# Straight code for the middle batches of a vision tower, and one GpSimd step moved behind a Newton step

## The reference, cut to what matters

```python
# 1 token mixer
y = sigmoid(q) * (ew @ (exp(k) * v)) / (ew @ exp(k))
h = y @ out_w + out_b + x
h = (h - mean) * rsqrt(var + 1e-5) * ln_g + ln_b      # first norm: scale ln_g, offset ln_b
h = concat([cls_tok, h])                              # a class row in front of the 256 tokens
# 2 attention with 16 heads, whose probabilities are mixed over the heads and normalised
attn = softmax(q @ k.T * scale)
attn = einsum('bhij,hg->bgij', attn, reattn_w)
attn = (attn - mean_over_heads) * rsqrt(var_over_heads + 1e-3) * gamma + beta
h = h + (attn @ v) @ w_out + b_out                    # q, k, v from layernorm(h)
# 3 feed-forward with ternary weights and activations rounded to 8 bits
h = h + bitlinear(silu(bitlinear(ln(h), w_gate)) * bitlinear(ln(h), w_up), w_down)
```

## Time and profile before

| | |
|---|---|
| median of three runs | 874.68 us |
| the profiled execution, its own time | 874.84 us |
| its span, first to last instruction | 873.1 us |
| mean granted TensorE clock | 0.935 of full speed |
| busy: PE, DVE, ACT, POOL | 84%, 74%, 50%, 21% of the span |
| instruction packets on the two instruction queues | 18 and 16 |

### The profile page before, as it was taken

One profiled execution on the slowest core, in us unless ns is written; L12 is line 12 of the kernel. 1 busy time (PEld: TensorE's weight loads), 2 busy tenths in 40 slices (PEclk: granted clock), 3 DMA queues, 4 the chain that ended last, 5 costly groups with the idle time before them and its releaser, 6 DMA issues.

```text
span 873.1 us, 14228 instructions
## 1 busy us (share of the span) xinstructions
PE 732.1 (84%) x4514; PEld 527.8 (60%) x4514; DVE 642.9 (74%) x1442; ACT 435.2 (50%) x1198; POOL 179.6 (21%) x367
## 2 busy tenths in 40 slices
PE   1769688989998999898998999899998899788754
PEld 0446466757675777666775767477766677456521
DVE  1596758688958896888768885889688886868444
ACT  0103637563657364745747265836575574747210
POOL 0308124012310233013301231023301330013000
PEclk9959799989999999989998999899999999899877
DMA  8300410050003200230004000311023000500000
GB/s 330 129 1 0 172 46 2 17 175 9 31 1 129 72 30 0 85 107 12 24 28 164 6 30 0 128 64 36 0 73 119 13 1 28 166 7 7 1 12 0
DMA packets 25414, 49.26 MB, mean 56 GB/s; under 512 B 2715, under 2 KB 6052, under 8 KB 24740
## 3 DMA queue, kind: packets, MB, share of 16 engines
q1 hardware_dynamic: 24340, 45.34, 15.4%
q10 hardware_dynamic: 1040, 3.49, 1.0%
HBM read 13.16 MB, written 2.11 MB: 17 GB/s over the span
## 4 chain that ended last, share of the span: by engine, by line
PE 37%; issue 26%; DVE 16%; ACT 8%; POOL 8%; DMA 4%; POOLq 1%; SPq 0%; ACTq 0%; DVEq 0%
PE small L535 5%; PE big L535 5%; PE small L686 5%; PE big L552 5%; DMA pg<-pst 4%; PE big L618 4%; DVE pst L1186 3%; DVE mx L1193 2%; ACT pst L918 2%; PE big L716 2%; PE small L641 2%; PE small L671 2%; ACT ot L1007 2%; DVE var L1221 1%; POOL nww L1569 1%
## 5 line engine op out<-in xcount | busy, mean ns | idle before, releaser
L918 ACT ACTIVATE pst<-big,nb 128x256 f32<-128x256 f32 x256 | 117.7, 473 | 46.9 <-DVE nb L1196 24.5
L618 PEld LDWEIGHTS big<-w_mix,pg 128*128 128x128 f32 x1024 | 122.5, 194 | 25.9 <-DVE an L1265 18.3
L618 PE MATMUL big<-w_mix,pg 128*128 128x128 f32 x1024 | 126.3, 279 | 7.9 <-DVE an L1265 7.9
L1193 DVE TENSOR_REDUCE mx<-big 128x4 f32<-128x1024 f32 x64 | 78.2, 1222 | 26.2 <-PE big L552 25.7
L552 PE MATMUL big<-qk_t 64*128 64x256 f32 x512 | 72.6, 402 | 20.1 <-ACT qk_t L901 20.1
L939 ACT ACTIVATE sqb<-big 128x1024 f32<-128x1024 f32 x64 | 64.8, 1014 | 42.9 <-PE big L618 42.9
L1221 DVE TENSOR_REDUCE var<-sqb 128x64 f32<-128x1024 f32 x64 | 77.6, 1213 | 9.1 <-ACT sqb L939 9.1
L1265 DVE TENSOR_TENSOR an<-big,rstd 128x1024 f32<-128x1024 f32 x64 | 78.4, 1225 | 2.7 <-DVE rstd L1252 0.2
L1186 DVE TENSOR_SCALAR pst<-pst,rr 128x256 f32<-128x256 f32 x256 | 72.8, 350 | 0.0
L552 PEld LDWEIGHTS big<-qk_t 64*128 64x128 f32 x512 | 44.2, 186 | 45.6 <-ACT qk_t L901 27.9
L535 PE MATMUL small<-xnt,w_qkv 128*128 128x256 f32 x256 | 65.5, 400 | 0.0
(11 more groups left out here) (200 smaller groups left out, 1233.5 us busy)
## 6 DMA issues: line engine op xcount, KB each, us to landing
pg<-pst SPq DMA_DIRECT2D x128, 256.0 KB
w_qkv<-in_w_qkv SPq DMA_DIRECT2D x1, 3072.0 KB
xt<-in_x_t SPq DMA_DIRECT2D x8, 256.0 KB, 2.9
xr<-in_x_tok SPq DMA_DIRECT2D x8, 256.0 KB, 2.7
out<-h SPq DMA_DIRECT2D x16, 128.0 KB
an<-in_gate_t ACTq DMA_DIRECT2D x1, 1024.0 KB, 8.5
an<-in_up_t ACTq DMA_DIRECT2D x1, 1024.0 KB, 10.8
an<-in_down_t ACTq DMA_DIRECT2D x1, 1024.0 KB, 13.3
```

The costliest lines, as they stand in the source:

```text
L618: last = mm(mix_place(n)[:, i * P:(i + 1) * P], pg[:, hf * (IB // 2) + i, it * T + jt * P:it * T + (jt + 1) * P], w_mix[:], start=True, st ...
L918: last = A(pst[:, g % 2, h % GH, it, :], big[p % 2][:, (j * TT + it) * T:(j * TT + it + 1) * T], ACT.Exp, bias=nb[:, h, it:it + 1], scale= ...
L1193: V.reduce_max(mx[:, hs, :], big[p % 2][:, :].rearrange("p (h t l) -> p h t l", h=2, t=TT), AX)\
```

## The change

The five hardware loops become Python loops, so that the instructions of iterations 1 to 5 (on SP 1 to 4) are written out, with constants in place of registers. On POOL, g and b leave `mixer_out` for a function of their own, `mixer_affine`. It is called for batch b + 1 behind `newton(b, 0)`, where it stood for batch b + 2 at the end of iteration b. Batch 0 keeps its place in the setup.

```diff
-            with sp.Fori(1, B - 3) as b:
+            for b in range(1, B - 3):
                 iteration(b, True, True)
...
-            with pe.Fori(1, B - 2) as b:
+            for b in range(1, B - 2):
                 iteration(b, True, True)
...
             def mixer_out(b):
                 power(b, pool_a, dve_a, ve_a, rs_a, P, slice(0, TT), "ve")
+
+            def mixer_affine(b):
                 pool.wait_ge(dve_a.sem, dve_a.at(b, ("n", 1)))
                 G.tensor_tensor(h2[:], h2[:], tok_g[:].unsqueeze(1).to_broadcast([P, TT, M]), ALU.mult)\
                     .then_inc(pool_a.sem, 1)
...
                 for n in mixes:
                     newton(b, n)
-                    if n == 3 and do_scores:
+                    if n == 0 and do_scores:
+                        mixer_affine(b + 1)
+                    elif n == 3 and do_scores:
                         mixer_norm(b + 1)
...
             mixer_out(0)
+            mixer_affine(0)
             mixer_norm(0)
```

More of the change, by code:

```diff
@@ L1073, in _ @@
             iteration(0, True, True)
-            with act.Fori(1, B - 2) as b:
+            for b in range(1, B - 2):
                 iteration(b, True, True)
@@ L1496, in _ @@
             iteration(0, True, True)
-            with dve.Fori(1, B - 2) as b:
+            for b in range(1, B - 2):
                 iteration(b, True, True)
@@ L1653, in _ @@
             iteration(0, True, True)
-            with pool.Fori(1, B - 2) as b:
+            for b in range(1, B - 2):
                 iteration(b, True, True)
```

## The result

The changed kernel takes 883.54 us (median of 14 runs, 877.12 to 1080.16) where the kernel before takes 875.76 (median of 14). The ratio is 1.0072, with a 95% interval of 1.0052 to 1.0092: slower by about 6.3 us (4.6 to 8.1). The two medians by themselves lie 7.8 apart, inside that interval. The forecast was 879.5, with a range of 875.0 to 884.0.

The account below looks back on a forecast made before the run. At the seam between iterations PE was taken to wait on a chain through DVE, POOL and ACT. Straight code -2.4, hold-off +5.75 and clock +1.53 gave +4.88 us: 879.5 against the median, range 875.0 to 884.0.

Parts of the forecast that it names:

- the hold-off: Block 0 at seams before iterations 1 to 6: g, issued first, holds off DVE's `rstd`; 5.75 us in all, chance 0.80.
- PE's wait: Ahead of PE's block 3 at the seam: the wait grows from 1.05 us to about 2.
- lateness at the seam is priced in full: Between iterations: block 3 later by 1.53 us makes the next `an` later by the whole 1.53; nothing is absorbed.
- Iteration 0: Its start: y * y begins 1.03 us sooner without g and b ahead; the hold on `rstd` takes it to 0.0.
- The straight code: Five iterations leaving the loop: less register arithmetic ahead of waits, 2.4 us saved; bounds 0 and 4.8.
- The third piece: From the start of `rstd` to `an`: straight code saves 0.11 us, only as long as `rstd` is short.
- The first piece: From the first `an` to that of block 7: 24.43 us in the loop, 24.15 straight, saving 0.28.
- The second: From block 7 to the next first `an`: 70.03 us in the loop, 69.83 straight, saving 0.20.
- The clock: At the seams, ahead of PE's block 3: one further fall, 1.53 us; bounds none and four (6.1).
- The rival by which a taken branch costs a fetch: Loop seams: the loop hid more than straight pieces show, over 2 us for each iteration needed; chance 0.03.
- the 0.90 and 0.91 of the forecast: Start of `hq` to `rstd`: 0.90 us with a taken branch, 0.91 where the loop is left; branch worth nothing.
- fetching straight code stalls: Rival on the written-out iterations: fetching their code stalls an engine, making the kernel slower; chance 0.02.

Follow-up runs that it names:

- e3: Changed kernel plus a wait that lets g go only when `rstd` of block 0 has ended: 876.35 us, 1.0001 to the kernel before.
- e1: Kernel before with all five loops written out, g and b left where they were: 876.68 us, 1.0002 to the kernel before.
- e4: Changed kernel with g and b each as two instructions of 128 x 256 values: 878.43 us, 1.0033 to the kernel before.
- e9: Changed kernel with g and b behind the Newton step of block 1, not block 0: 881.54 us, 1.0067 to the kernel before.
- e5: e3 plus a second wait, letting block 7's `rstd` go ahead of POOL's copy: 877.28 us, 1.0013 to the kernel before.
- e2: Changed kernel with the five hardware loops kept, so the moved step alone: 883.98 us, 1.0090 to the kernel before.
- e13: Changed kernel plus twelve unread 128 x 512 products on PE per iteration from 1 on: 879.05 us, 1.0048 to the kernel before.
- e10: e1 plus twelve unread 128 x 512 products on PE per iteration from 1 on: 870.44 us, 0.9952 to the kernel before.
- e11: e10 plus five more unread products between the gate and the up projection: 868.00 us, 0.9914 to the kernel before.
- e12: Kernel before, loops kept, plus twelve unread 128 x 512 products on PE per iteration from 1 on: 870.50 us, 0.9943 to it.

## Why the prediction was right, and where it was not

- **The place, the cause and the size of the hold-off: right.** 1.28 us was forecast for `rstd` and 1.27 measured, 0.07 behind g where 0.08 was forecast; 1.31 from `rstd` to `an`, and 316.83 - 315.53 = 1.30 measured. g holds alone; b costs `an` and POOL's queue nothing. Undoing it (e3) gave back 6.2 us, against the 5.75 of the sum. The traces of the changed kernel and e1 say the same: from the start of the first `rstd` to the second `an` of an iteration it takes 1.31 + 4.89 = 6.20 us with the hold and 0.26 + 4.99 = 5.25 without, so 0.95 at each of six seams, with 1.03 in iteration 0 some 6.7 in all. Lateness at the seam is thus carried on all but for 0.10.
- **PE's wait: about 2 us forecast, 1.80 measured.** That lateness at the seam is priced in full holds but for the 0.10 for block 0 (e3, e4), and less closely for block 1 (e9). It does not carry over to block 7 (e5), where the earlier trace rows show the same hold: there the hold, 0.8 us longer than `rstd` alone, has no price that can be measured.
- **Iteration 0: right.** `y` ends at 124.40 and y * y now starts at 124.48, 0.08 behind it and not 1.11, and the hold takes that back. The first `an` is 0.39 later than before, of which `y` itself came 0.37 later, out of the setup.
- **The straight code: mis-sized, -2.4 forecast, 0 measured** (1.0002, 0.9976 to 1.0028, so between 2.1 us less and 2.5 more). The third piece, 0.11 between `rstd` and `an`, is lost again by the next `an` (e1), as said above. The first piece came: 24.16 us from the first `an` to block 7 in the changed kernel, for 24.43. The second, 0.20 behind block 7, did not: in the profiled executions of before and after that stretch is longer in each of iterations 0 to 5, by 0.9 to 1.2 us in four of them and by 2.1 and 2.5 in 1 and 5, where the fall of the clock grew; the hold at the next seam is 0.94 of it. The piece had been read from iteration 0 alone, at equal clock by choice, while the clock there was the one thing that would not stay equal.
- **The clock: the wrong place, and for a reason that did not hold.** One fall more at a seam, 1.53 us, was in the sum, because PE's wait there would double. The wait grew to 1.80, and in the profiled execution no seam has a fall. The falls behind block 7 grew in iterations 1 and 5 instead, 48 to 51 us in all. In e2 the falls came at three seams, and in e1 and e3, with the shortest wait, at one. What the clock does is thus an outcome of each version's timing that these rows could not give; the runs of one kernel already spread by 0.925 to 0.940.
- **The fetches.** The rival by which a taken branch costs a fetch that straight code gives back is out at the size that it needed, over 2 us for each iteration: 1.0002 in e1. A fetch of some tenths of a microsecond at four seams is too small for that ratio to show; against it stand only the 0.90 and 0.91 of the forecast. That fetching straight code stalls is not seen either: the packets rose from 18 and 16 to 36 and 28 and no wait is put down to them.
- **The sum**, +4.88, was short of the measured 6.3 by 1.4. The straight code was credited with 2.4 too much, the clock charged with up to 1.5 too much, and the hold-off with 0.45 too little: 2.4 - 1.5 + 0.45 = 1.35. This is bookkeeping over separate measurements, each good to some 2 us. That the time fell into the range is in part luck: the straight code and the clock were both misjudged, in opposite directions, and 883.54 lies only 0.5 below the upper end, also because the kernel before came out at 875.76 this time and not at 874.68.

What stays open: which of the small shifts sets how long the clock falls behind block 7; and why the hold-off looks larger, some 8 us, when e2 is compared with the kernel before, or e13 with e10 (1.0048 against 0.9952), or the changed kernel with e3 once their clocks of 0.932 and 0.927 are brought together by the fitted line. In e2 the three falls at seams are part of it; for e13, whose runs have 0.947 of the clock and e10's 0.951, clock is 2 us of it by the fitted line, and the 6 left are about what e3 gives for the hold-off.

## What to carry to other kernels

Before a GpSimd instruction is moved, see which DVE instruction will start just behind it. If that one reads two tiles in SBUF and GpSimd's reads SBUF, the DVE one lasts as long as GpSimd's, and a wait that lets the short one go first cost nothing that could be measured (e3). What such a hold costs is read from what comes behind it: seven holds of 1.05 us cost 6 us at the seam, and seven of 0.8 cost nothing measurable at block 7, where the engine goes on to wait for another anyway. And a small saving next to a stretch in which PE waits and its clock falls can't be counted on: price it at several iterations with different clock, and keep PE at work in those waits (e11).

## What was not expected of the hardware

- **The falls of the clock cost about as much as the change**: filling PE's waits with products nobody reads took 0.5 to 0.9% off (e10 to e12), with a mean granted clock of 0.951 to 0.954 in place of 0.933.
- **A gap of 0.07 to 0.09 us decides.** After POOL's product both POOL's next instruction and DVE's waiting `rstd` are ready, and POOL's starts 0.07 to 0.09 ahead in every row shown here, although g carries a wait of its own, long satisfied. A wait on `rstd` itself turned the order round. Once it turned by itself, at block 7 of iteration 5 in e4, where `rstd` starts 0.01 ahead, keeps its 0.23, and the copy takes 1.11 in place of 1.04:

```profile
623.77 0.23 DVE L1252 SCALAR_TENSOR_TENSOR rstd<-nww,y 128x64 f32<-128x64 f32 x1
623.78 1.11 POOL L1520 TENSOR_TENSOR xnv<-xnt,ones 128x512 f32<-128x512 f32 x1
```

- **The same chain is held up the other way round as well.** Just ahead of `rstd` at the seam, POOL's y * y takes 0.76 us and its x * y * y 0.77, where elsewhere they take 0.29 and 0.32. Each starts while one of DVE's two steps over 128 x 1024 values is running, `sqb` rounded (line 1356) or `hq` (line 1360), and ends 0.15 to 0.18 behind it:

```profile
311.48 0.75 DVE L1356 TENSOR_SCALAR sqb<-sqb,s2u 128x1024 f32<-128x1024 f32 x1
```

  It is so at all seven seams of the kernel before, of the changed one and of e1, and at no other block, with 0.68 to 0.77 for x * y * y. These two DVE steps read one tile each, so a single SBUF input leaves POOL free in some DVE steps, such as `an`, and not in all, as the forecast had it. That is 0.8 to 0.9 us on the chain at each seam, nearly as much as the hold by g; no run tried another order there.
- **Register work in a loop is hidden by a longer instruction**: `an` follows `rstd` by 0.37 us from start to start in the loop with `rstd` at 0.23, by 0.26 in straight code.
